# The y of two groups turned, joined and split chunk by chunk inside the attention and kept in DRAM; the adapter's low products first; new orders in the first steps

## What is computed

```python
h    = einsum('bct,bcd->bdt', x, style_w[style_id])          # 32x32 matrix per sequence
qkv  = clip(einsum('bsd,ed->bse', h, w_qkv), -8, 8)
q, k = layer_norm(q) * w + b, layer_norm(k) * w + b           # over 512
p    = softmax(where(causal, q @ k.T / 4 + alibi, -inf))      # 32 heads of 16
x1   = x + (p @ v) @ w_out.T
y    = einsum('bsi,boi->bso', x1, w2[adapter_id])             # 512x512 matrix per sequence
gate = sum(top_2(y @ gate_w))                                 # of 8
f    = relu(y @ up_w)**2 @ down_w + gate * (y @ route)        # up 512x1024, route = fc1 expert fc2
out  = x1 + layer_norm(f) * gamma + beta
```

## Time and profile before

| | us |
|---|---|
| median of 3 runs | 1165.56 (1161.65 to 1165.74) |
| the profiled execution | 1165.9 |
| its span, first to last instruction | 1164.1 |
| TensorE busy | 1103.2 (95%) |
| VectorE busy | 696.3 (60%) |
| ScalarE busy | 602.2 (52%) |
| POOL busy | 711.1 (61%) |
| mean granted clock of TensorE | 0.986 |

### The profile page before, as it was taken

The page is one execution under the profiler, slowest core; times in us unless marked ns, Lnnn a source line. Parts: engine busy times, 40 slices in busy tenths (PEclk is TensorE's granted clock), DMA queues, the critical chain, the costliest instruction groups (busy, mean ns, idle before and its releaser), DMA issues.

```text
span 1164.1 us, 27353 instructions
## 1 busy us (share of the span) xinstructions
PE 1103.2 (95%) x10996; PEld 895.4 (77%) x10996; DVE 696.3 (60%) x1058; ACT 602.2 (52%) x1001; POOL 711.1 (61%) x610
## 2 busy tenths in 40 slices
PE   6889999999999999999987999999999999999994
PEld 3667788888788888888875778787888878787883
DVE  5657676666566666666677546555656554544432
ACT  4355776767677777666665532617162533424120
POOL 4345788878788787878664545645545455533332
PEclk9989999999999999999999999999999999999998
DMA  7014555555555555464467833151423313130101
GB/s 268 30 56 152 182 174 180 173 186 180 172 171 193 181 178 187 131 189 124 160 167 202 286 115 108 64 144 64 125 79 91 95 64 88 58 82 28 46 28 36
DMA packets 90796, 152.38 MB, mean 131 GB/s; under 512 B 46000, under 2 KB 46768, under 8 KB 85296
## 3 DMA queue, kind: packets, MB, share of 16 engines
q1 hardware_dynamic: 73024, 105.84, 29.0%
q0 software_dynamic: 12224, 34.10, 9.7%
q10 hardware_dynamic: 5424, 10.71, 2.8%
HBM read 89.78 MB, written 38.27 MB: 110 GB/s over the span
## 4 chain that ended last, share of the span: by engine, by line
PE 84%; DMA 6%; issue 4%; DVE 4%; ACT 1%; SPq 1%; POOL 0%; DVEq 0%; POOLq 0%
PE bank L592 18%; PE pair L768 15%; PE bank L744 15%; PE bank L681 9%; PE bank L761 8%; PE bank L632 6%; DMA w2t<-in_w 4%; PE bank L582 3%; PE pair L654 2%; PE bank L640 2%; PE pair L609 2%; PE bank L714 1%; PE bank L667 1%; PE bank L620 1%; DVE words_first L1280 1%
## 5 line engine op out<-in xcount | busy, mean ns | idle before, releaser
L1620 POOL TENSOR_TENSOR w_lo<-w2t,w_hi 128x2048 fp32r<-128x2048 f32 x38 | 175.4, 4615 | 30.0 <-ACT w_hi L924 29.4
L592 PE MATMUL bank<-wqkv_hi,h_hi 128*128 128x512 f32 x384 | 154.8, 403 | 0.3
L1678 POOL TENSOR_TENSOR u_lo<-act,u_hi 128x512 fp32r<-128x512 f32 x64 | 83.3, 1302 | 110.0 <-ACT u_hi L1107 109.8
L592 PE MATMUL bank<-wqkv_lo,h_hi 128*128 128x512 f32 x384 | 150.0, 391 | 0.0
L592 PE MATMUL bank<-wqkv_hi,h_lo 128*128 128x512 f32 x384 | 149.9, 390 | 0.0
L744 PE MATMUL bank<-yT_hi,up_hi 128*128 128x512 f32 x256 | 101.2, 395 | 1.0 <-DVE yT_lo L1287 1.0
L768 PE MATMUL pair<-down_hi,u_hi 128*128 128x512 f32 x256 | 100.9, 394 | 0.0
L768 PE MATMUL pair<-down_hi,u_lo 128*128 128x512 f32 x256 | 100.8, 394 | 0.0
L768 PE MATMUL pair<-down_lo,u_hi 128*128 128x512 f32 x256 | 100.3, 392 | 0.0
L744 PE MATMUL bank<-yT_hi,up_lo 128*128 128x512 f32 x256 | 100.0, 390 | 0.0
L744 PE MATMUL bank<-yT_lo,up_hi 128*128 128x512 f32 x256 | 99.8, 390 | 0.0
(11 more groups left out here) (181 smaller groups left out, 2959.1 us busy)
## 6 DMA issues: line engine op xcount, KB each, us to landing
w2t<-in_w SPq DMA_DIRECT2D x38, 1024.0 KB
vx<-v_hl SPq DMA_DIRECT2D x128, 68.0 KB
x_rows<-x1t SPq DMA_DIRECT2D x32, 256.0 KB, 4.0
x1g<-x_rows SPq DMA_DIRECT2D x32, 256.0 KB, 3.0
kx<-k_hl SPq DMA_DIRECT2D x124, 64.0 KB
ffn_high<-w_high SPq DMA_DIRECT2D x20, 256.0 KB, 3.0
ffn_low<-w_low SPq DMA_DIRECT2D x20, 256.0 KB, 2.4
stage<-in_wqkv SPq DMA_DIRECT2D x3, 1024.0 KB, 8.0
```

Source lines behind the costliest of these rows:

```text
L592: m = e.matmul(into, a[:, c, :], b[:, n, c, :], start=(c == 0 and k == 0), stop=(c == KC - 1 and k == 2))
L1620: e.tensor_tensor(w2_lo[:, :, :], w2t[:, :, :], w2_hi[:, :, :].bitcast(F32), ALU.subtract).then_inc(d_wlo, 1)
L1678: e.tensor_tensor(u_lo[n % FC][:, :], act[n % 2][:, :], u_hi[n % FC][:, :].bitcast(F32), ALU.subtract) \
```

## The change

1. `EARLY_GROUPS = 2`: y of groups 0 and 1 is treated inside the attention, one chunk `j` (0 to 7) in each of the last eight steps. SP loads the two halves of the next chunk into `planes` (transposing), ScalarE joins them in one instruction (`join_planes`) and rounds (`high_planes`), VectorE subtracts (`low_planes`), SP stores both parts to DRAM (`keep_planes`). In the passage SP reads them back into `yT_hi`, `yT_lo` (`load_back`): six transfers for group 0, two for group 1. The old joins, roundings and subtractions of both groups go, and so do the tiles `words_first`, `words_second`, `yt_first`. Later groups are joined by one instruction instead of two.
2. In `adapt_slot` the four products with `w2_lo` come first; after them `load_w2` of the next slot may start (`d_wl`). `high_w2` gets a wait for the end of the products.
3. ScalarE does the chunk (and the planes) of a step ahead of `high_w2`.
4. In the first four steps POOL makes `style_bd` right after its gathers, TensorE does `style(i+1)` ahead of `project_q(i)`, ScalarE does `high_h` ahead of `high_probs`; in steps 3 to 5 POOL does `low_probs` ahead of `reciprocals`.
5. In the passage `high_k(T-1)` and `low_k(T-1)` come earlier, and the second `fetch_up` comes after `high_u(0)`.

```diff
+EARLY_GROUPS = 2
+    y_parts = [nc.dram_tensor(f"y_part_{n}", [EARLY_GROUPS * KC, P, GROUP * P], F32, kind="Internal").ap()
+               for n in ("high", "low")]
+    planes = fsb("planes", [P, 2, TOK], U16)
+    y_word = fsb("y_word", [P, TOK])
+    y_high = fsb("y_high", [P, TOK], F32R)
+    y_low = fsb("y_low", [P, TOK], F32R)
...
@@ SP
             def load_w2(s):
                 if s:
-                    e.wait_ge(d_m, s)
+                    e.wait_ge(d_wl, s)
...
+            def load_planes(j):
+                m, c = j // KC, j % KC
+                rows = slice(TOK * m, TOK * m + TOK)
+                if j:
+                    e.wait_ge(p_word, j)
...
+                for n in range(2):
+                    cols = slice(DM * n + P * c, DM * n + P * c + P)
+                    e.dma_start(planes[:, n, :], y_rows[rows, cols], transpose=True).then_inc(p_in, 16)
+
+            def keep_planes(j):
+                e.wait_ge(p_high, j + 1)
+                e.dma_start(y_parts[0][j], y_high[:, :].bitcast(F32)).then_inc(p_kept, 16)
+                e.wait_ge(p_low, j + 1)
+                e.dma_start(y_parts[1][j], y_low[:, :].bitcast(F32)).then_inc(p_kept, 16)
+
+            def load_back(m, part, first_, last_):
+                e.wait_ge(p_kept, 32 * (KC * m + last_))
+                dst = (yT_hi, yT_lo)[part][m][:, first_:last_, :]
+                e.dma_start(dst.bitcast(F32), y_parts[part][KC * m + first_:KC * m + last_].rearrange("c p n -> p c n")) \
+                    .then_inc(p_back[m], 16)
...
-                if T - 6 <= i < T - 2:
-                    load_y(0, (i - T + 6,))
+                if i >= T - 8:
+                    keep_planes(i - T + 8)
+                if i >= T - 9:
+                    load_planes(i - T + 9)
...
             store_x1(T - 6)
-            load_y(1, (0, 1))
+            upto(e, "x1", T - 6)
+            load_back(0, 0, 0, 3)
+            keep_planes(EARLY_GROUPS * KC - 1)
+            upto(e, "tq", T - 2)
+            load_back(0, 1, 0, 1)
+            upto(e, "tk", T - 2)
+            load_back(0, 1, 2, 3)
             spread_k(T - 2)
             load_w2(slot_up(0))
+            upto(e, "tq", T - 1)
+            load_back(0, 1, 1, 2)
+            upto(e, "tk", T - 1)
+            load_back(0, 1, 3, 4)
             spread_v(T - 3)
             store_x1(T - 5)
+            load_back(0, 0, 3, 4)
             spread_k(T - 1)
...
-            load_y(1, (2, 3))
...
             store_x1(T - 2)
+            upto(e, "r", T - 1)
+            load_back(1, 0, 0, KC)
+            load_back(1, 1, 0, KC)
             store_x1(T - 1)
@@ TensorE
-                for c in range(KC):
-                    for k, (a, b) in enumerate(((xgT_hi, w2_hi), (xgT_hi, w2_lo), (xgT_lo, w2_hi))):
-                        m = e.matmul(into, a[:, P * c:P * c + P], b[:, c, :], start=(c == 0 and k == 0),
-                                     stop=(c == KC - 1 and k == 2))
+                pairs = [(xgT_hi, w2_lo, c) for c in range(KC)]
+                pairs += [(a, w2_hi, c) for c in range(KC) for a in (xgT_hi, xgT_lo)]
+                for k, (a, b, c) in enumerate(pairs):
+                    m = e.matmul(into, a[:, P * c:P * c + P], b[:, c, :], start=(k == 0), stop=(k == len(pairs) - 1))
+                    if k == KC - 1:
+                        m.then_inc(d_wl, 1)
...
+            def y_ready(m):
+                if m < EARLY_GROUPS:
+                    e.wait_ge(p_back[m], 96 if m == 0 else 32)
...
             for i in range(T - 1):
+                if 0 < i < SHORT:
+                    style(i + 1)
                 project_q(i)
-                if i < SHORT:
-                    style(i + 1)
+                if i == 0:
+                    style(1)
@@ ScalarE
+            def join_planes(j):
+                e.wait_ge(p_in, 32 * (j + 1))
+                if j:
+                    e.wait_ge(p_low, j)
+                e.activation(y_word[:, :].bitcast(U16).rearrange("p (t n) -> p t n", n=2),
+                             planes[:, :, :].rearrange("p n t -> p t n"), ACT.Copy).then_inc(p_word, 1)
+
+            def high_planes(j):
+                e.wait_ge(p_word, j + 1)
+                if j:
+                    e.wait_ge(p_kept, 32 * j)
+                e.activation(y_high[:, :], y_word[:, :], ACT.Copy).then_inc(p_high, 1)
...
             for i in range(T - 1):
-                if i >= 3:
-                    high_probs(i - 3)
                 if i < SHORT:
                     high_h(i + 1)
...
+                if i >= 3:
+                    high_probs(i - 3)
...
+                if 0 <= i - 5 < CHUNKS:
+                    high_chunk(i - 5)
+                if i >= T - 8:
+                    join_planes(i - T + 8)
+                    high_planes(i - T + 8)
                 if i >= LAG:
                     high_w2(i - LAG)
-                if 0 <= i - 5 < CHUNKS:
-                    high_chunk(i - 5)
...
             high_o(T - 4)
             high_probs(T - 3)
-            high_k(T - 1, B5, k_last)
             slot_out(LAST, B2)
-            high_y(0, 3)
...
-            e.wait_ge(S["lo"], KC)
-            fetch_up(m_up[1], 0, 1, 8)
-            fetch_up(m_up[1], 1, 1, 8)
...
             high_u(0)
+            fetch_up(m_up[1], 0, 1, 8)
+            fetch_up(m_up[1], 1, 1, 8)
@@ VectorE
+            def low_planes(j):
+                e.wait_ge(p_high, j + 1)
+                if j:
+                    e.wait_ge(p_kept, 32 * j)
+                e.tensor_tensor(y_low[:, :], y_word[:, :], y_high[:, :].bitcast(F32), ALU.subtract).then_inc(p_low, 1)
...
                 if 0 <= i - 5 < CHUNKS:
                     low_chunk(i - 5)
+                if i >= T - 8:
+                    low_planes(i - T + 8)
                 take_k(i)
...
             stats_of(T - 1, 0, qn, "cq")
-            join_y(0, 0)
-            join_y(0, 1)
+            low_planes(EARLY_GROUPS * KC - 1)
             take_k(T - 1)
...
             low_o(T - 4)
+            low_k(T - 1, B5, k_last)
             bias_max(T - 2)
-            low_k(T - 1, B5, k_last)
-            low_y(0, 3)
@@ POOL
                     gather_style(i + 3)
+                if i < SHORT:
+                    style(i + 2)
                 if i >= LAG:
                     low_w2(i - LAG)
+                if 3 <= i < LAG:
+                    low_probs(i - 3)
                 reciprocals(i)
-                if i >= 3:
+                if i >= LAG:
                     low_probs(i - 3)
...
-                if i + 2 < T:
+                if i >= SHORT and i + 2 < T:
                     style(i + 2)
```

More of the change, by code:

```diff
@@ L367, in program @@
     m_route, m_down = sem("m_route"), sem("m_down")
+    p_in, p_word, p_high, p_low, p_kept = (sem(f"p_{n}") for n in ("in", "word", "high", "low", "kept"))
+    p_back = [sem("p_back0"), sem("p_back1")]
+    d_wl = sem("d_wl")
     d_zero, d_w2, d_x = sem("d_zero"), sem("d_w2"), [sem("d_x0"), sem("d_x1")]
@@ L394, in turns @@
     def turns(m, f):
-        if m:
-            return (f - 2,) if 0 <= f - 2 < KC else ()
-        return range(KC) if f == EARLY else ()
+        return (f - 2,) if m and 0 <= f - 2 < KC else ()
     def slot_at(m):
@@ L479, in load_y @@
                 for s in (last_slot(m) - 1, last_slot(m)):
                     e.wait_ge(d_y[s % 2], 16 * (s // 2 + 1))
-                for c in chunks:
-                    if m == 1:
-                        e.wait_ge(S["word"], c + 1)
+                for c in range(KC):
                     for n in range(2):
                         cols = slice(DM * n + P * c, DM * n + P * c + P)
-                        e.dma_start(rows_of(m)[:, c, n, :], y_rows[rows, cols], transpose=True) \
-                            .then_inc(f_y, 16)
+                        e.dma_start(yt[:, c, n, :], y_rows[rows, cols], transpose=True).then_inc(f_y, 16)
@@ L570, in _ @@
                 if m + 2 < GROUPS:
-                    load_y(m + 2, range(KC))
+                    load_y(m + 2)
         @block.tensor
@@ L729, in up @@
                 if f == 0:
-                    e.wait_ge(S["lo"], KC * (m + 1))
+                    y_ready(m)
                 if n == 0:
@@ L1113, in _ @@
             high_probs(T - 4)
+            join_planes(EARLY_GROUPS * KC - 1)
+            high_planes(EARLY_GROUPS * KC - 1)
             high_w2(LAST)
@@ L1274, in add_x @@
                 e.tensor_tensor(x1t[t % 2][:, :], B6, xt[t % XR][:, :], ALU.add).then_inc(A["x1"], 1)
[L1276 to L1281 removed]
+            def low_planes(j):
[3 more added lines that the diff above has]
+                e.tensor_tensor(y_low[:, :], y_word[:, :], y_high[:, :].bitcast(F32), ALU.subtract).then_inc(p_low, 1)
             def low_y(m, c):
[L1284 to L1286 removed]
+                e.wait_ge(S["hi"], KC * (m - EARLY_GROUPS) + c + 1)
                 e.tensor_tensor(yT_lo[m % 2][:, c, :], words(m, c), yT_hi[m % 2][:, c, :].bitcast(F32),
@@ L1499, in _ @@
             low_o(T - 2)
-            for c in range(KC):
```

(1 more changed line is left out.)

67 lines of the change are left out of this document (23 added, 44 removed).

## The result

The changed kernel takes 1144.4 us in the median (1143.2 to 1145.2), the kernel before 1163.6 us beside it on the same chip (1158.8 to 1165.7): a ratio of 0.984, 95% interval 0.980 to 0.988. The profiled execution of the changed kernel has a span of 1142.1 us, that of the kernel before 1164.1, so 22.0 us are gone. The prediction was 1140 with a range of 1132 to 1152. The total is 4.4 us off. The parts are further off than that and in both directions, as the table by stage shows, so part of the hit is luck.

The account below looks back on a forecast made before the run. TensorE was taken as the bound, so time could come only from its 61 us of idleness and its slow-clock stretches. Gains of 8.9 + 5.2 - 1.5 + 13.0 = 25.6 us off 1165.9 gave 1140, range 1132 to 1152.

Parts of the forecast that it names:

- the start: First attention steps, reordered around `style`: 8.9 us gained from idle time and slow clock, bounds 7 and 10.5.
- the steps of the loop: Attention steps behind the start: 5.2 us gained in seven slower steps, 1.5 lost to the planes in the last eight.
- the passage: Way from attention to FFN: 13.0 us gained from idle time and three slow stretches, bounds 8.5 and 17.
- The 0.8 before `project_k(2)`: First steps: a pause of 0.8 us (0 to 1.5) on TensorE, waiting for `q_lo(0)`.
- The steady steps: Seven slower steps go from 19.64 to 18.90 us as `w_low` no longer stands behind w2's transfer: 5.2 us gained.
- The planes: Last eight steps, extra join, rounding and subtraction for y: 1.5 us lost, between 0 and 4; join put at 1.3.
- the feared loop lateness: Last eight steps: late `w_lo` delays `subtract_max`, the exponential, `p_hi` and the next join, so lateness grows step by step.
- The slower rival: Last eight steps: the planes' subtraction collides with POOL's `w_lo`, seven steps of 4.5 us more; 1176 us, chance 6%.
- The 6 us of the passage: Slower rival's extra: the passage, hit by the same collision, keeps its 4.5 us pause and 1.5 of slow clock.
- 1.0, 0.7 and 1.5: Passage pauses expected to stay: 1.0 us before `up(0,0)`, 0.7 before `out_project`, 1.5 inside `values` with no releaser.
- the last store: Passage: x1's last store, behind 2.1 MB of group 1, delays the adapter's products; 4.2 us taken, between 0.6 and 7.2.
- The crowded rival: Passage transfers crowd one another: `kx` keeps its 4.3 + 1.6 and the last store pays in full; 1149 us, chance 22%.

Follow-up runs that it names:

- e7_fetch_early: Changed kernel with the 2 MB of the second `fetch_up` issued ahead of `soft_exp(T-2)`, right behind the last `kx` spread: 1147.8 us, 0.9875 of the kernel before.
- e9_chunk_but_last: Changed kernel with ScalarE's chunk put behind `high_w2` in every step except that of the last chunk: 1144.9 us, 0.9836 of the kernel before.

## Why the prediction was right in sum and wrong in a part

The sum came out right because errors of both signs met: the start gave 0.9 us more than predicted, the steps of the loop 3.0 more (6.7 against 5.2 - 1.5), the passage 7.5 less. That they leave only 3.6 is luck.

- **The start.** Predicted 8.9, measured 9.8. The pause before the first `turn_q` was put at 2.3 and is 2.00 (41.34 us, `turn_q` waiting for `kn`); the one before `values(0)` at 1.5 and is 1.58. The 0.8 before `project_k(2)` doesn't exist; that is the difference. No slow stretch followed the 2.0.
- **The steady steps.** Predicted 5.2 for seven steps at 18.90; they take 18.91. The size was right. The cause given was not: the argument was that `w_low` no longer queues behind w2's transfer, and the runs show that this edit and the earlier load can both be undone without the steps getting longer. A wait that the trace of before shows as last link was taken for the cause, though the transfer behind it was itself late. What shortens the steps stays open.
- **The planes.** Predicted 1.5 of loss, none seen: the join takes 1.166 us where 1.3 stood, 0.10 above the lower bound of the earlier trace rows, and the feared loop lateness does not appear; the steps stay at 18.9. The margin between `y_low` and `w_lo` is 1.0 us in the last step and 0.5 in the one before. The slower rival, 1176, had the right mechanism, and its condition is met when `y_low` falls behind `high_w2`; its price was too high. The run lost 18 us, not 31.5 + 6. It put 3.0 us of pause and 1.5 of slow clock on each of seven steps; TensorE paused 13.1 us in them (the two rows of that run less the 2.2 of the start), 1.9 a step and never more than 1.3 at once, and the steps took 20.6 to 22.5 us instead of 18.9. The 6 us of the passage were not tried, since that run leaves the last `y_low` where it was (0.68 us).
- **The passage.** Predicted 13.0, measured 5.5. This is the step that failed. `take_v` goes on at once, `kx` is there in time (2.41 us of issue, no pause), and the pauses that remain beside the store's are 1.7 (for `vx`, which the prediction didn't have), 1.3 (without a releaser) and 0.4 where 1.0, 0.7 and 1.5 stood; that the sums agree is chance. The term that was mis-sized is the last store: 4.2 was taken for it, "what it costs today", and it costs 8.7 and a slow stretch of 2.5, 11.2 together. That is 7.0 of the 7.5 missing. Even the prediction's upper bound, 7.2, was too low: it let the store wait for the 5.2 us that 2.1 MB take at 408 GB/s, but the loads share those 400 GB/s with ScalarE's queue, which moves `route` and `down_lo` there. SyncE's queue moved only 0.33 of 2.04 MB from 633 to 638 us, and 1.29 of 2.01 in the next 5 us. The store landed 13.7 us after its issue, 8.3 more than the 5.4 that it took with nothing in front of it on its own queue. The rule of the Trainium skill that the prediction weighed, DMA: Bandwidth & Descriptors (Queues, rings and completion order), was the better guide: by that reading the store pays in full, and it did, with more than the 5.2.
- **The crowded rival** had 1149 with the store in full and `kx` late. Half of it came true, the store; the other half did not. The value of 4.2 was chosen because the row was of this very pause, but in the kernel before that pause had another cause (the roundings and subtractions in front of it, the last of which run from 667.62 to 671.10 us, when the store had already landed at 667.3), so its length said nothing of the new one. The bound from the bandwidth row was nearer, and the queue's small share of the bandwidth is the term that the prediction lacked.

## What to carry to other kernels

Before a large load is put on a queue, list the small transfers issued behind it and who waits for them; a small store whose reader is on the critical path goes first, since moving two lines was worth 10 us here. When a new VectorE operation reads two SBUF tiles, find the POOL operations that read SBUF beside it and place it before them; its own 0.7 us say nothing about what it costs if it starts one microsecond later. And if a wait is removed and the time improves, undo that edit alone before crediting it.

## What the runs showed of the hardware

- A store of 256 KB lands 5.4 us after its issue while the DMA engines move 400 GB/s for another queue, and 13.7 us after it when 2.1 MB stand in front on its own queue. The total rate is the same in both.
- VectorE's 512-column subtraction with both operands in SBUF takes 0.68 us alone and 3.5 to 4.4 us when it starts beside POOL's 4.6 us `w_lo`; `w_low`, with one operand in PSUM, starts beside the same `w_lo` and keeps its 0.69.
- ScalarE's one activation that interleaves two planes of 512 halfwords takes 1.166 us, less than the 2 x 0.776 us of the two strided ones that it replaces.
- With two queues full, the share of each changes: while ScalarE's queue still had `route_lo` and the 2 MB of `down_lo` under way, SyncE's queue moved 0.33 MB (ScalarE's 1.45) in its first 5 us and 1.29 MB (ScalarE's 0.70) in the next 5.
- The length of a pause alone doesn't say whether the clock falls. In the changed kernel a pause of 2.0 us in the first steps was followed by a granted clock of 1.00, one of 8.7 us by 5.2 us at 0.51. In its second trace a pause of 2.1 us before 593.9 us was followed by 2.6 us at 0.50. The 1.7 us of `e7_fetch_early` was followed by 0.50 as well, while the 2.7 us of `e9_chunk_but_last` was followed by 1.00.
- Pauses of 1.0 to 2.7 us without a releaser come behind the start at a few fixed places: at a `kx` product in the step of the first slot (in the kernel before and four runs), at the last adapter product of slot 25 (in the changed kernel, its second trace and six runs), and once each at a late `vx` and `kx` product. Four traces have none of them. No run explains them, so a difference of 1 to 3 us between single traces is not to be credited to an edit.
